# Block 0's first chunk by pairs of row tiles, its inner product copied by ScalarE and weighed by VectorE, in a new order of stages

## The reference

```python
x = x + 0.5 * ffn(layernorm(x))
x = x + attention(layernorm(x))      # 16 heads of 16, causal, k and q layer-normed per head
x = x + 0.5 * ffn(layernorm(x))

def ffn(x):                          # 6 experts of rank 16, the best 2 of them
    base, shared = x @ base_W.T + base_b, (x @ shared_A.T) @ shared_B.T
    gate = softmax(x @ router_W.T + router_b)
    w = gate where it is among the top 2, else 0;  w /= sum(w) + 1e-6
    routed = sum over e of w[e] * (x @ routed_A[e].T) @ routed_B[e].T
    return base + shared + routed
```

## Time and profile before

| | |
|---|---|
| median of 3 runs | 1140.63 us (1139.14 to 1141.39) |
| the profiled execution | 1141.34 us, its span 1139.5 us |
| TensorE busy | 1059.9 us (93%) |
| ScalarE busy | 1031.8 us (91%) |
| VectorE busy | 451.5 us (40%) |
| POOL busy | 235.9 us (21%) |
| mean granted clock of TensorE | 0.986 |

### The profile page before, as it was taken

How to read it: one execution, slowest core, us unless ns; L and a number is a source line. 1 busy time by engine, 2 the same in 40 slices (tenths; PEclk the granted TensorE clock), 3 DMA queues, 4 the chain that set the end, 5 groups by cost and what they waited for, 6 DMA issues and landing times.

```text
span 1139.5 us, 22310 instructions
## 1 busy us (share of the span) xinstructions
PE 1059.9 (93%) x8692; PEld 336.0 (29%) x8692; DVE 451.5 (40%) x1159; ACT 1031.8 (91%) x1163; POOL 235.9 (21%) x384
## 2 busy tenths in 40 slices
PE   3869899999999999999999999999999999999995
PEld 3644242232222232322222323322222232232123
DVE  6966556533234245343423243525013323223005
ACT  5457989999999999999999999999999999989991
POOL 3156343232213012130120130112013010010100
PEclk9988999999999999999999999999999999999998
DMA  5143425042004310142201042100004112111000
GB/s 118 37 131 110 96 80 135 11 125 45 20 15 136 84 29 11 35 125 66 39 1 10 19 113 57 34 15 19 15 10 118 37 33 53 38 29 28 11 10 28
DMA packets 93973, 60.59 MB, mean 53 GB/s; under 512 B 56434, under 2 KB 91240, under 8 KB 93864
## 3 DMA queue, kind: packets, MB, share of 16 engines
q1 hardware_dynamic: 91732, 59.00, 20.1%
q10 hardware_dynamic: 2132, 0.12, 0.1%
HBM read 23.97 MB, written 22.28 MB: 41 GB/s over the span
## 4 chain that ended last, share of the span: by engine, by line
PE 68%; ACT 12%; DVE 7%; issue 5%; DMA 4%; POOL 2%; SPq 1%; ACTq 0%; DVEq 0%; POOLq 0%
PE ps L1519 66%; ACT ring L1074 11%; DMA xnT<-area 3%; PE ps L1648 1%; POOL ring L991 1%; DVE st L1114 1%; DVE area L1168 1%; DMA keys_d<-split 1%; SPq L800 1%; POOL rstd L977 1%; POOL split L732 1%; DVE area L1143 0%; DVE area L1165 0%; DMA x<-in_x 0%; DVE x L1301 0%
## 5 line engine op out<-in xcount | busy, mean ns | idle before, releaser
L1074 ACT ACTIVATE ring<-ps 128x1024 f32<-128x1024 f32 x1056 | 985.3, 1087 | 41.2 <-PE ps L1519 38.7
L1519 PE MATMUL ps<-ring,vf 128*17 128x512 f32 (+3 forms) x4608 | 544.7, 564 | 4.2 <-POOL ring L991 3.1
L1519 PE MATMUL ps<-queries,keys 50*128 50x512 f16 (+3 forms) x2304 | 357.3, 366 | 29.1 <-ACT ring L1074 8.8
L1519 PEld LDWEIGHTS ps<-queries,keys 50*128 50x128 f16 x2304 | 90.1, 93 | 466.2 <-ACT ring L1074 414.1
L991 POOL TENSOR_SCALAR_AFFINE_SELECT ring<-ring 128x256 f32<-128x256 f32 (+1 forms) x224 | 101.2, 471 | 269.2 <-ACT ring L1074 265.7
L1519 PEld LDWEIGHTS ps<-ring,vf 128*17 128x17 f32 x4608 | 88.7, 96 | 198.6 <-issue 157.4
L1301 DVE SCALAR_TENSOR_TENSOR x<-ps,power,x 128x512 f32<-128x512 f32 x32 | 24.0, 750 | 180.7 <-PE ps L1519 180.2
L1482 DVE STREAM_TRANSPOSE oT<-ps 128x512 f32<-128x512 f32 x32 | 22.9, 716 | 76.8 <-PE ps L1519 76.7
L1519 PE MATMUL ps<-qkT,xnT 128*128 128x512 f16 x192 | 48.5, 381 | 2.7 <-DMA xnT<-area 1.1
L977 POOL TENSOR_TENSOR rstd<-var,minus_half 128x4 f32<-128x4 f32 x23 | 23.8, 1038 | 129.9 <-DVE var L1120 129.8
L1519 PE MATMUL ps<-baseT,xnT 128*128 128x256 f16 x360 | 49.3, 275 | 0.1
(11 more groups left out here) (176 smaller groups left out, 637.1 us busy)
## 6 DMA issues: line engine op xcount, KB each, us to landing
queries<-queries_d SPq DMA_DIRECT2D x64, 100.0 KB
queries_d<-split SPq DMA_DIRECT2D x48, 128.0 KB
keys_d<-split SPq DMA_DIRECT2D x48, 128.0 KB
keys<-keys_d SPq DMA_DIRECT2D x32, 192.0 KB, 3.4
x<-in_x SPq DMA_DIRECT2D x8, 512.0 KB, 4.2
out_x<-x SPq DMA_DIRECT2D x16, 256.0 KB, 2.1
x_d<-x SPq DMA_DIRECT2D x5, 512.0 KB, 4.4
att_d<-xnT SPq DMA_DIRECT2D x5, 512.0 KB, 2.6
```

The source lines that it names most:

```text
L1074: act.activation(probs[:, u % RING, :], bank(2 * (u % SLOTS), 2), ACTF.Exp, bias=0.0, scale=1.0).then_inc(exp_ok, 1)
L1519: return pe.matmul(o, lhsT, rhs, start=start, stop=stop, skip_group_check=True)
```

## The change

- The first and the second norm of chunk 0 go by pairs of row tiles, as the last chunk's third norm did: moments, power and bias once for each pair. `norms_done` counts them for the waits.
- TensorE's inner product of chunk 0 waits for each turned half just before the two row tiles that it serves.
- ScalarE copies chunk 0's inner result out of PSUM (line 1067), right after the exponential of its routing; VectorE does the weighing.
- PRELUDE, PLACES and HELD are new as a whole. Written out as a list, some stages stand elsewhere: in the prelude, sizes 0 stands between the moments of pair 0 and pair 1; weight 2 ahead of chunk 0's second turned half; chunk 1's last routing step ahead of chunk 0's first residual, weight 3 ahead of its second, weights 4 and 5 ahead of both biases of the second norm; chunk 1's second aggregates behind the four head norms of chunk 0; chunk 2's last routing step and the addition of bo to chunk 0 ahead of POOL's squares of chunk 1; fetch (0,1) directly behind fetch (0,0), the spill of chunk 0 and the load of chunk 4 around fetch (0,2), weigh0 2 near the end.

Beside the units (before, after, by the number of the unit whose exponential stands ahead):

| stage | before | after |
|---|---|---|
| turnin0 2 | 5 | 2 |
| heads (1,0), (1,2), (1,1), (1,3) | 7, 9, 11, 14 | 7, 10, 11, 16 |
| turn0 (3,1), inner0 3 | 37, 41 | 35, 41 |
| turn1 (3,1), first qk of chunk 3 | 81, 88 | 88, 91 |
| turn0 (6,1), inner0 6 (first half) | 436, 437 | 434, 436 |
| projout (3,1), inner1 3 (first half) | 831, 848 | 836, 854 |
| projout (4,1), inner1 4 (first half) | 883, 899 | 887, 907 |
| moments2 (5,1), inner1 5 (first half) | 921, 936 | 934, 952 |
| moments2 (6,1), inner1 6 (first half) | 963, 979 | 995, 1010 |

```diff
--- before.py
+++ after.py
@@ -48,6 +48,8 @@
 START_BANKS = (7, 5, 4, 3)
 END_BANKS = (7, 0, 1, 2, 3, 4, 5)
 NW = 7
+SPLIT_NORMS = ((0, 0), (1, 0), (2, NC - 1))
+SPLIT_INNER = (("inner0", 0), ("inner1", NC - 1))
 BLOCKS = (0, 2, 1, 3)
 FETCH = 2 * 16
 FLAG_STEPS = 9
@@ -242,83 +244,83 @@
 PRELUDE = (
-    "ffffwgffwgwgfffwgfgfgwfgggfggfppwgphwwgpphppgppppprpppphppppppprppppprhrhhppwqrrhphhprrrrrqrrpqh"
-    "qrrrrrpp"
+    "fwfffggwwfwfgffgfgfgfwfggggfgpwfpgwwpphgpppgpppppphrppphppppppppphppprrhhwprprqqhhhrpphrprrrrprr"
+    "qprrrrqhr"
 )
...
 PLACES = {
-        (0, "prep"): (0, 0, 0, 3, 3, 4, 17, 17, 17, 21, 28, 33, 42, 49, 50),
-        (0, "ff"): (6, 17, 40, 50),
+        (0, "prep"): (0, 0, 0, 0, 0, 4, 4, 7, 8, 21, 32, 35, 48, 53, 59),
+        (0, "ff"): (6, 46, 51),
...
@@ -440,7 +442,12 @@
         return n == NC - 1
     if stage == "heads":
         return n[0] < SCALAR_HEADS
-    return stage == "qk" and n // TC <= 2 or (stage, n) == ("inner1", NC - 1)
+    return stage == "qk" and n // TC <= 2 or (stage, n) in SPLIT_INNER
+
+
+def norms_done(ln, c, a):
+
+    return sum(2 if (ln, m) in SPLIT_NORMS else 1 for m in range(c)) + (1 + a if (ln, c) in SPLIT_NORMS else 1)
 
 
 def high_heads(k):
@@ -961,18 +968,18 @@
             pool.wait_ge(const, NCONST)
 
             for stage, n in ORDER:
-                if stage == "weigh0":
+                if stage == "weigh0" and n > 0:
                     weigh(pool, main, 0, n)
                 elif stage == "weigh1" and n < NC - 1:
                     weigh(pool, main, 1, n)
-                elif stage == "moments2" and n[0] == NC - 1:
-                    c, a = n
-                    pool.wait_ge(main.var_ok[2], c + 1 + a)
-                    q = norm_set(main, 2, c)
-                    pool.tensor_tensor(rstd[q][:, 2 * a:2 * a + 2], var[q][:, 0, 2 * a:2 * a + 2], minus_half[:, :].broadcast_to([P, 2]), ALU.pow).then_inc(main.rstd_ok[2], 1)
+                elif stage in ("moments0", "moments1", "moments2") and (int(stage[-1]), n[0]) in SPLIT_NORMS:
+                    ln, (c, a) = int(stage[-1]), n
+                    pool.wait_ge(main.var_ok[ln], norms_done(ln, c, a))
+                    q = norm_set(main, ln, c)
+                    pool.tensor_tensor(rstd[q][:, 2 * a:2 * a + 2], var[q][:, 0, 2 * a:2 * a + 2], minus_half[:, :].broadcast_to([P, 2]), ALU.pow).then_inc(main.rstd_ok[ln], 1)
                 elif stage in ("moments0", "moments1", "moments2") and n[1] == 1:
                     ln = int(stage[-1])
-                    pool.wait_ge(main.var_ok[ln], n[0] + 1)
+                    pool.wait_ge(main.var_ok[ln], norms_done(ln, *n))
                     q = norm_set(main, ln, n[0])
                     pool.tensor_tensor(rstd[q][:, :], var[q][:, 0, :], minus_half[:, :].broadcast_to([P, TC]), ALU.pow).then_inc(main.rstd_ok[ln], 1)
                 elif stage == "square":
@@ -1026,7 +1033,7 @@
                     act.activation(dst, src, ACTF.Copy).then_inc(main.w_high, 1)
                 elif stage in ("scale0", "scale1") and n[0] < SCALAR_SCALES[int(stage[-1])]:
                     ln, (c, a) = int(stage[-1]), n
-                    act.wait_ge(main.nm_ok[ln], c + 1)
+                    act.wait_ge(main.nm_ok[ln], norms_done(ln, c, a))
                     q = norm_set(main, ln, c)
                     for i in range(2):
                         t = 2 * a + i
@@ -1045,7 +1052,7 @@
                     act.activation(split[:, 0, k % 2, :], bank(main.bank[stage, n]), ACTF.Identity, bias=scaled[:, g + 1:g + 2], scale=scaled[:, g:g + 1])
                     act.activation(qT[k % 2][:, :], bank(main.bank[stage, n]), ACTF.Identity,
                                    bias=scaled[:, g + 1:g + 2], scale=scaled[:, g:g + 1]).then_inc(main.read_act, 1)
-                elif stage in BANK_STAGES and on_scalar(stage, n) and stage != "inner1":
+                elif stage in BANK_STAGES and on_scalar(stage, n) and (stage, n) not in SPLIT_INNER:
                     if stage == "qk" and n < TC * SCALAR_SQUARES:
                         squares_free(act, main, n)
                         act.wait_ge(main.ready, main.use[stage, n])
@@ -1094,8 +1101,11 @@
 
             def moments(K, ln, c, k):
                 own, x, q = K.own, K.x(c, ln), norm_set(K, ln, c)
-                if K is main and (ln, c) == (2, NC - 1):
-                    dve.wait_ge(*K.done["projout", (c, k)])
+                if K is main and (ln, c) in SPLIT_NORMS:
+                    if ln == 0:
+                        dve.wait_ge(*K.x_in(c))
+                    else:
+                        dve.wait_ge(*K.done["outer0" if ln == 1 else "projout", (c, k)])
                     for i in (2 * k, 2 * k + 1):
                         dve.bn_stats(st[q][:, i, :], x[:, i, :]).then_inc(*own.up())
                     dve.wait_ge(*own.at())
@@ -1130,9 +1140,12 @@
                 x, q = K.x(c, ln), norm_set(K, ln, c)
                 dve.wait_ge(*K.own.at())
                 if K is main:
-                    dve.wait_ge(K.rstd_ok[ln], c + 1 + (a if (ln, c) == (2, NC - 1) else 0))
+                    dve.wait_ge(K.rstd_ok[ln], norms_done(ln, c, a))
                 if K is main and c < SCALAR_SCALES[ln]:
-                    if a == 0:
+                    if (ln, c) in SPLIT_NORMS:
+                        dve.scalar_tensor_tensor(out=var[q][:, 1, 2 * a:2 * a + 2], in0=mv[q][:, 2 * a:2 * a + 2, 0], scalar=-1.0,
+                                                 in1=rstd[q][:, 2 * a:2 * a + 2], op0=ALU.mult, op1=ALU.mult).then_inc(K.nm_ok[ln], 1)
+                    elif a == 0:
                         dve.scalar_tensor_tensor(out=var[q][:, 1, :], in0=mv[q][:, :, 0], scalar=-1.0, in1=rstd[q][:, :],
                                                  op0=ALU.mult, op1=ALU.mult).then_inc(K.nm_ok[ln], 1)
                     return
@@ -1469,8 +1482,8 @@
 
             for stage, n in ORDER:
                 front_and_heads(main, stage, n)
-                if (stage, n) == ("weigh1", NC - 1):
-                    weigh(dve, main, 1, n)
+                if (stage, n) in (("weigh0", 0), ("weigh1", NC - 1)):
+                    weigh(dve, main, int(stage[-1]), n)
                 elif stage == "gather":
                     if n == 0:
                         dve.wait_ge(ones_in, 32)
@@ -1576,11 +1589,12 @@
                 b = side_bank(K, key, 0 in parts)
                 if 0 in parts:
                     pe.wait_ge(K.w_ok, 1)
-                if c == NC - 1:
-                    wait_turned(K, 2 * f, c, parts)
-                elif 0 in parts:
+                apart = K is main and (f"inner{f}", c) in SPLIT_INNER
+                if 0 in parts and not apart:
                     wait_turned(K, 2 * f, c)
                 for i in [2 * k + j for k in parts for j in range(2)]:
+                    if apart and i % 2 == 0:
+                        wait_turned(K, 2 * f, c, (i // 2,))
                     for ib in range(2):
                         m = mm_parts(b[:, i * NA:(i + 1) * NA], lambda s: turned_rows(K, 2 * f, c)[:, i, s, ib, :], lambda s: aT[:, s, ib, :],
                                      i == 0 and ib == 0, i == TC - 1 and ib == 1)
```

More of the change, by code:

```diff
@@ new lines @@
+        185, 190, 196, 207, 207, 207, 213, 213, 214, 228, 240, 257, 257, 257, 257, 257, 258, 261, 279, 292, 324, 324, 339, 340, 356, 372,
+        389, 405, 421),
+        (4, "out"): (0, 22, 41),
+        (4, "back"): (72, 74, 79, 79, 92, 105, 125, 145, 148, 148, 148, 214, 242, 242, 244, 251, 267, 277, 290, 304, 317, 330, 343),
+        (5, "prep"): (0, 1, 18, 20, 31, 44, 48, 58, 61, 73, 73, 74, 94, 106, 122, 139, 145, 147, 147, 154, 159, 160, 162, 185, 195, 198,
+        212, 217, 222, 239, 242, 242, 243, 257, 277, 292, 300, 308, 310, 317, 319, 320, 320, 324, 342, 360, 382, 382, 382, 384, 474, 493,
@@ new lines @@
+        499, 518, 538),
+        (5, "out"): (24, 24, 26),
+        (5, "back"): (60, 70, 73, 75, 87, 95, 95, 95, 115, 116, 117, 124, 257, 266, 281, 296, 312, 329, 365, 387, 411, 437, 452),
+        (6, "prep"): (0, 0, 4, 5, 42, 55, 65, 76, 77, 87, 88, 104, 110, 139, 139, 155, 169, 170, 173, 173, 174, 178, 194, 209, 218, 229,
+        229, 229, 229, 230, 245, 246, 254, 258, 264, 264, 264, 265, 279, 287, 287, 296, 296, 296, 316, 329, 332, 333, 333, 353, 355, 447,
+        581, 603, 635),
+        (6, "out"): (12, 27, 31, 32, 46, 57),
@@ new lines @@
+        (6, "back"): (61, 62, 87, 94, 116, 116, 129, 129, 129, 129, 232, 281, 307, 307, 312, 312, 313, 364, 382, 392, 435, 483, 546),
+        (7, "out"): (0, 19, 19, 19, 28, 28),
+        (7, "back"): (29, 36, 49, 51, 66, 72, 76, 94, 96, 103, 106, 106, 127, 127, 133, 139, 144, 150, 156, 165, 172, 183, 191, 196, 206,
+        220, 220, 226, 227, 227, 227, 227, 227, 256, 286, 286, 288, 297, 300, 303, 308, 311, 330, 336, 348, 361, 361, 367, 374, 389, 400,
+        414, 420, 426, 426, 435, 445, 448, 455, 463, 480, 498, 531, 540, 549, 559, 568, 582, 586, 596, 607, 612, 613, 631, 635, 637, 640,
```

(23 more changed lines are left out.)

61 lines of the change are left out of this document (16 added, 45 removed).

## The result

The kernel after takes **1128.92 us** (median of 4 runs, 1127.33 to 1130.21) against 1140.41 us of the kernel before beside it (4 runs, 1139.14 to 1141.39): ratio 0.9897, 95% interval [0.9882, 0.9912], so 11.7 us less, between 10.0 and 13.5. The forecast was 1136.6 with a range down to 1132.5: the direction was right, the size three times too small. The profiled execution took 1127.33 us around a span of 1125.6.

A forecast was written before the change was run, and what follows sets the result against it. TensorE and ScalarE were both taken as the bound, so only time in which both stand still can be won. Prelude and block 0 -2.0 plus later landings -2.0 made -4.0: 1140.6 to 1136.6 us, range 1132.5 to 1142.

The forecast's parts named there:

- the later landings: Blocks behind block 0: two waits before second feed-forward inner products go, -2.5; chunk 6's inner product +0.5; sum -2.0.
- bounds -2 and +3, taken as 0: New orders in all blocks may bring new waits that no row shows; priced at 0 within these bounds.
- Prelude and block 0: From the start through block 0: late prelude set against the queries' wait removed; -2.0 together, bounds -4 and +0.5.
- Pair steps: Prelude up to chunk 0's inner product: the first norm by pairs brings the logits at 22.0, +1.1.
- +1.7 for everything behind: End of chunk 0's norms in the prelude, 59.3 instead of 57.59, passed on to all later; bounds 0 and +3.5.
- The fetch: Block 0: group 1's queries, fetched right behind group 0's, are there by 75 to 76, so TensorE's wait goes.
- for POOL's weighed tile at turnin0 2: Block 0: chunk 2's weighing ends at 80.5, so TensorE stands from 78.3 to 80.5.
- Heads (1,0): Block 0: chunk 1's last norm is ready at 87.9, TensorE comes to them at 88.4 instead of 90.43.
- leaves those 8 us at the lower one: Block 0: the sum keeps TensorE's clock at 1.2 GHz there, because stops remain.
- Rival A: Slower: prelude later than block 0 can win, from +3.7; sign first scores after 78; 1143 us; chance 0.17.
- C: More gain: clock stays at 2.4 GHz in block 0 and prelude is on time; 1133 us; chance 0.10.
- B: No change: block 1's start hangs on chunk 1's keys and queries, removed waits return elsewhere; 1139.6 us; chance 0.27.

The follow-up runs named there:

- four stops filled: Kernel after with unread 512-column matmuls (13, 8, 9 and 16) in four stops of TensorE: 1129.36 us, ratio 0.9894.
- without the first norm's pairs: Kernel after without pair steps of chunk 0's first norm, its halved inner wait and ScalarE's copy, with POOL weighing; second norm's pairs stay: 1131.42 us, ratio 0.9921.
- the new code alone: Kernel before in its old order, old PRELUDE and tables, with the new pair, halved-inner, copy and weighing code: 1141.60 us, ratio 1.0009.
- run with the stop filled: Kernel before with 26 unread 512-column matmuls inside block 0's stop of 6.2 us ahead of scores 5: 1134.22 us, ratio 0.9957.
- all new tables: Kernel before with PLACES and HELD of blocks 1 to 7 from the kernel after; prelude and block 0 old: 1132.12 us, ratio 0.9928.
- blocks 1 to 3: Kernel before with PLACES and HELD of the kernel after in these blocks only: 1136.40 us, ratio 0.9964.
- blocks 4 to 7: Kernel before with PLACES and HELD of the kernel after in these blocks only: 1135.45 us, ratio 0.9949.
- block 7: Kernel before with PLACES and HELD of the kernel after in this block only: 1139.24 us, ratio 0.9994.
- consumers later: Kernel before with five stages that wait for transposed rows, and their other halves, moved about three units later: 1143.96 us, ratio 1.0029.
- HELD alone: Kernel before with only the table of held value batches of blocks 1 to 7 from the kernel after: 1149.58 us, ratio 1.0095.
- PLACES alone: Kernel before with only the new places of blocks 1 to 7, its old held batches kept: 1141.42 us, ratio 0.9999.

## Why the prediction was wrong in size, point by point

**The step that failed: "the later landings", -2.0, measured -8.2.** The forecast read the list of waits, found 5.9 us of waits for transposed rows, priced the two largest, and gave all else in the new tables "bounds -2 and +3, taken as 0", because "new waits no row shows". The two waits did go (the inner products near 960 and 1002 of after follow without a stop). Three things were wrong in it. The gain does not lie where it was looked for: all the waits for transposed rows together are 5.9 us, and moving their consumers away lost 3.3; the largest share, about 2.5 us, is in block 1, where the list has one such wait of 1.1. The forecast had no term for what the new order does to the waits between ScalarE and TensorE: 27.4 us one way and 8.4 the other stood in the same list, six times the 5.9. And HELD, named as changed, got no price at all, although alone it costs 10.8. The bound of -2 was no bound: nothing in the rows excluded a larger gain, since 35.8 us of mutual waits stood there.

**Prelude and block 0: -2.0 forecast, -2.1 measured [-3.8, -0.3], by other sizes.** The sum is right by luck: two errors cancel.
- Pair steps: +1.1 at the logits was +0.4, +1.3 at the turned result +0.4, +2.0 at the first qk +1.1, +1.7 at the norms +0.7. Each time the walk came out 0.7 to 1.0 us too late.
- "+1.7 for everything behind" failed: the first scores were +3.9. The walk stopped at chunk 0 and charged nothing for chunk 1's second norm in the new order, in which TensorE stood 1.87 and 2.19 us and ran the inner products and part of the qk at the half clock.
- The fetch: right, no wait for queries is left. No wait "for POOL's weighed tile at turnin0 2" was seen (80.33); with first scores that late the tile was there. With first scores at 75.79, in the run with four stops filled, there was one, of 0.51.
- Heads (1,0) forecast at 88.4, found at 86.69; that the sum "leaves those 8 us at the lower one" was wrong. The granted clock of block 0 was 1.00 throughout. Taking the idling out of the old stop gave 4.9 us, more than the whole forecast for block 0. The last norm of chunk 1 was forecast at 87.9; in five kernels heads (1,0), which need it, run at 87.3 to 88.2 after standing for it, so in these it is what comes last there.
- Rival A's rule, that a late prelude passes one for one into block 0, holds one way only. First scores 2.7 us later (without the first norm's pairs) came with a first gather 2.9 later, and 2.5 later (the new code alone) with 1.9; but with the four stops filled first scores 1.8 us earlier left the first gather where it was (0.2 later), because VectorE's norm comes last at heads (1,0).

**The rivals.** C was the nearest: the clock stayed up in block 0, though it put the prelude on time, which it was not. B's mechanism appeared, with 1.80 us at block 1's start, when the fetch alone was moved. A's time did not come, although the first scores at 77.62 nearly reached its mark of 78. The Trainium skill, TensorE: Matmul & The Clock Gate, section "HAM oscillation — how this bites in real kernels", charges a stretch at the lower level with half its length; from 82.73 to about 91 that is an estimate of 4.1 us. The run with the stop filled agrees, with 4.9 [2.4 to 7.4].

**What the pair code itself gives** is not settled: nothing in the old order (+1.0, with an interval that holds 0). In the new order taking out the first norm's part cost nominally 2.7 us, with overlapping intervals, and its trace agrees in direction (first scores 2.7 us later, block 0's end 3.8). A kernel without any of it came to 1130.6.

**What stays open.** The mutual waits of ScalarE and TensorE, summed both ways from 111 to 1100 us, are 35.8 us in the trace of before, but 32.5 to 34.1 in the four others with its tables of blocks 1 to 7. By run: all new tables 25.2 (time -8.2), blocks 1 to 3 30.6 (-4.1), blocks 4 to 7 31.4 (-5.8), block 7 33.8 (-0.7), consumers later 39.1 (+3.3), HELD alone 51.1 (+10.8), PLACES alone 44.5 (0.0, with 1.8 for transposed rows in place of 5.9). So kernels far apart differ in the same direction in both, while the small steps are within what one trace differs from the next, and PLACES alone breaks the order. The mutual waits go with most of the gain; that they cause it is argued and not shown, since ScalarE's wait for scores also grows when TensorE stands for something else, as before 1002.23. No run changed the alignment of a single batch. That block 1's gain comes from the places, and which blocks lose when one table is changed alone, the traces show; which entries do it was not tried.

## What to carry to other kernels

Where two engines are both near 90% busy, look in the list of waits at what they wait for each other, and not only at the waits that have a conspicuous releaser: the former were six times the latter here, and the forecast that had no term for them was 6 us short. Two tables that fix one order are best tried together and apart, and compared block by block: a total near 0 hid some 4 us won and 7 lost. Behind a long stop of TensorE look at the granted clock before asking how to shorten the stop; unread matmuls in it are a cheap way to measure what the clock is worth.

## What the runs showed of the hardware

- After the stop of 6.21 us in block 0 the granted clock was 0.50 for some 8 us; filled with unread matmuls, the same stop cost 4.9 us less of 1141.
- The half clock also stands behind shorter stops, though not behind each: in the kernel after, the eight matmuls at 58.42 behind a stop of 2.21 take 1.06 us (1.94 in before, behind a stop of 3.53), while stops of 1.87 and 2.19 us stand ahead of stretches with these clocks (columns: from:to, length, TensorE busy, granted clock, DMA share, GB/s):

```profile
62.00:66.00 4.00, 4.00 (x39) 0.65 0.35 102
68.00:72.00 4.00, 3.62 (x10) 0.57 0.57 124
77.62:107.24 29.62, 26.09 (x276) 1.00 0.48 146
```

- A stop's aftermath differs from execution to execution: the inner product at 999.25 of before took 2.33 us behind a stop of 1.67, and 1.41 behind stops of 1.63 and 1.75 in two other kernels with the same tables there. Behind stops of 2.41 before heads (1,0) four matmuls took 1.09 us in the kernel with four stops filled and 0.63 in the kernel after with the old later tables. A single profile can be 2 to 3 us off over one block.
